# DLRM tower: nine tables by one-hot instead of eleven, compared three chunks at a time, and a paced row of gathers

## What is computed

```python
e = stack([tbl_f[ids[:, f]] for f in range(26)], axis=1)          # 512 x 26 x 128
c = concatenate([dense[:, None, :], e], axis=1)                   # 512 x 27 x 128
inter = einsum('bfd,bgd->bfg', c, c)[:, iu, ju]                   # 351 pairs, f < g
h = concatenate([dense, inter, dense], axis=1)                    # 607
h = maximum(h @ W_top1 + b_top1, 0)                               # 512
h = maximum(h @ W_top2 + b_top2, 0)                               # 256
y = h @ W_top3                                                    # 1
```

## Time and profile before

| | |
|---|---|
| median of 3 runs | 130.52 us (130.05 to 130.78) |
| the profiled execution | 131.74 us, of which the span of the profile is 129.6 us |
| TensorE busy | 111.9 us, 1026 matmuls |
| VectorE busy | 85.5 us, 168 instructions |
| ScalarE busy | 81.1 us, 172 instructions |
| GpSimd busy | 60.4 us, 68 instructions |
| DMA | 12.28 MB, mean 95 GB/s |

### The profile page before, as it was taken

How to read it: one execution, slowest core, us unless ns; L and a number is a source line. 1 busy time by engine, 2 the same in 40 slices (tenths; PEclk the granted TensorE clock), 3 DMA queues, 4 the chain that set the end, 5 groups by cost and what they waited for, 6 DMA issues and landing times.

```text
span 129.6 us, 2680 instructions
## 1 busy us (share of the span) xinstructions
PE 111.9 (86%) x1026; PEld 91.5 (71%) x1026; DVE 85.5 (66%) x168; ACT 81.1 (63%) x172; POOL 60.4 (47%) x68
## 2 busy tenths in 40 slices
PE   0389999999799999999696929999999986996892
PEld 0147776775667767758476919999798985995890
DVE  3379999999999999999991970952166032571001
ACT  6398198769888989999603750983167413582231
POOL 2478786485748771526667756656742000000000
PEclk9999999999999999999999995999999999999999
DMA  4937787574894636621111212112201000000000
GB/s 121 272 81 206 231 254 211 135 200 102 226 247 139 192 71 214 195 43 40 48 51 37 58 28 70 46 45 52 65 22 46 18 0 0 5 0 21 0 0 1
DMA packets 6681, 12.28 MB, mean 95 GB/s; under 512 B 2926, under 2 KB 3598, under 8 KB 6669
## 3 DMA queue, kind: packets, MB, share of 16 engines
q1 hardware_dynamic: 4605, 7.92, 22.3%
q0 software_dynamic: 1920, 3.94, 11.7%
q10 hardware_dynamic: 144, 0.26, 0.8%
HBM read 11.91 MB, written 0.00 MB: 92 GB/s over the span
## 4 chain that ended last, share of the span: by engine, by line
DVE 50%; PE 35%; issue 5%; DMA 4%; ACT 3%; SPq 2%; DVEq 0%
DVE hot L468 31%; PE ps L581 11%; DVE tab_lo L457 9%; PE ps L605 8%; DVE z L494 6%; PE ps L618 4%; PE ps L565 3%; DMA ids_i<-in_ids_dram 3%; PE ps L531 2%; DVE emb_t L486 2%; PE ps L551 2%; SPq L317 2%; PE ps L548 2%; ACT z L416 1%; DMA z<-z 1%
## 5 line engine op out<-in xcount | busy, mean ns | idle before, releaser
L342 POOL DMA_INDIRECT rows<-in_tbl_dram,ids_i x60 | 59.5, 992 | 36.9 <-DMA rows<-in_tbl_dram,ids_i 24.9
L468 DVE TENSOR_SCALAR hot<-ps,row_no 125x512 fp32r<-125x512 f32 x68 | 46.1, 748 | 1.0 <-PE ps L518 1.0
L551 PE MATMUL ps<-hot,tab_lo 125*128 125x512 f32 x92 | 38.0, 413 | 1.9 <-DVE tab_lo L457 1.9
L548 PE MATMUL ps<-hot,tab_hi 125*128 125x512 f32 x92 | 38.9, 423 | 0.8 <-ACT emb_t L389 0.8
L494 DVE COPY z<-ps 32x112 f32<-32x112 f32 (+1 forms) x64 | 16.5, 258 | 14.0 <-PE ps L581 13.2
L416 ACT COPY z<-ps 32x112 f32<-32x112 f32 (+1 forms) x64 | 15.2, 238 | 13.9 <-PE ps L581 13.2
L548 PEld LDWEIGHTS ps<-hot,tab_hi 125*128 125x128 f32 x92 | 18.4, 200 | 7.4 <-issue 2.1
L551 PEld LDWEIGHTS ps<-hot,tab_lo 125*128 125x128 f32 x92 | 18.3, 199 | 6.9 <-DVE tab_lo L457 3.2
L581 PE MATMUL ps<-emb_t 128*64 128x52 f32 x512 | 17.7, 232 | 4.8 <-DVE emb_t L486 3.6
L581 PEld LDWEIGHTS ps<-emb_t 128*64 128x64 f32 x512 | 17.0, 149 | 6.0 <-ACT emb_t L408 4.0
L605 PE MATMUL ps<-z,w_pair 128*128 128x128 f32 x128 | 16.6, 277 | 1.1 <-DMA z<-z 1.1
(11 more groups left out here) (42 smaller groups left out, 66.1 us busy)
## 6 DMA issues: line engine op xcount, KB each, us to landing
tab<-in_tbl_dram SPq DMA_DIRECT2D x9, 448.0 KB
tab<-in_tbl_dram SPq DMA_DIRECT2D x2, 560.0 KB
rows<-in_tbl_dram,ids_i POOLq DMA_INDIRECT x60, 3.1
w<-in_W_top_dram SPq DMA_DIRECT2D x1, 512.0 KB, 5.5
tab<-in_tbl_dram SPq DMA_DIRECT2D x9, 52.0 KB
x_rows<-in_r_dense_features_dram ACTq DMA_DIRECT2D x1, 256.0 KB, 3.3
w_x<-in_W_top_dram SPq DMA_DIRECT2D x1, 256.0 KB, 4.2
h_t<-in_W_top_dram SPq DMA_DIRECT2D x1, 256.0 KB, 4.5
```

Of the source, the lines that this page charges most:

```text
L342: pool.indirect_dma_start(out=rows[:, t, gathered.index(f), :], out_offset=None, in_=tables[f - 1], in_offset=bass.IndirectOffsetOnAxis(id ...
L468: nc.vector.tensor_scalar(hot[0:RP, k % OHB], ps[0:RP, IDV + n % 2, :], row_no[0:RP, row_cols(n, c)], None, ALU.is_equal).then_inc(hot_dve, 1)
L548: nc.tensor.matmul(bank, tab_hi[0:RP, n % SPLIT, c], one_hot, start=c == 0, stop=False)
L551: nc.tensor.matmul(bank, tab_lo[0:RP, n % SPLIT, c], one_hot, start=False, stop=c == CHUNKS[n] - 1).then_inc(hot_used, 1)
```

## The change

- Features 9 and 19 are gathered, not looked up by one-hot: 9 tables of 8 chunks remain; 17 features are gathered in 5 groups, 68 gathers. The groups are now (0 to 3), (12 to 15), (5 to 8), (9, 19, 20, 21), (23, 24).
- `ORDER`: g4 follows g3 in every tile, and g0:1 moves from between two tables to behind the last.
- VectorE compares chunks 0 to 2 and chunks 3 to 5 each in one `tensor_tensor` of 125 x 1536, with both inputs spread by a step of 0; the `tab_lo` of a table lies between the two. ScalarE builds chunks 6 and 7 (before: 3 and 6). One-hots have 16 buffers, two tables of 8.
- GpSimd waits at the head of each group for TensorE to have done a number of tables (group k of the whole row: k - 2 tables, up to 9), later for Gram units and first-layer blocks; the row of gathers in tiles 2 and 3 waits for the third before, not the second.

```diff
-ONEHOT = [4, 10, 11, 16, 17, 18, 22, 25, 26, 9, 19]
-GROUPS = [[(0, 4)], [(12, 4)], [(5, 4)], [(20, 2), (23, 2)]]
+ONEHOT = [4, 10, 11, 16, 17, 18, 22, 25, 26]
+GROUPS = [[(0, 4)], [(12, 4)], [(5, 4)], [(9, 1), (19, 3)], [(23, 2)]]
...
 ORDER = [
-    "h h g0:0 h g1:0 h g2:0 h g3:0 h h g0:1 h h h h",
-    "u0:0 g1:1 u1:0 g2-3:1 u0-1:1",
-    "g0-1:2 x0 l0-1:0 g2:2 l2-3:0 g3:2 e0 y0",
+    "h h g0:0 h g1:0 h g2:0 h g3:0 h g4:0 h h h",
+    "g0:1 u0:0 g1:1 u1:0 g2-4:1 u0-1:1",
+    "g0-1:2 x0 l0-1:0 g2:2 l2-3:0 g3:2 e0 g4:2 y0",
     "u0:2 x1 l0:1 u1:2 l1-3:1 g0:3 e1 g1:3 y1",
-    "x2 l0-1:2 g2-3:3 u0-1:3 x3 l2-3:2 e2 y2 l0-3:3 e3 y3",
+    "x2 l0-1:2 g2-4:3 u0-1:3 x3 l2-3:2 e2 y2 l0-3:3 e3 y3",
 ]
...
-    ACT_CHUNKS = [(3, 6) if m == R8 else (2, 5, 8) for m in CHUNKS]
-    DVE_CHUNKS = [tuple(c for c in range(m) if c not in a) for m, a in zip(CHUNKS, ACT_CHUNKS)]
-    OHB = 10
+    DVE_PARTS = [(0, 3), (3, 6)]
+    ACT_CHUNKS = (6, 7)
+    OHB = 2 * R8
...
-        return s[0] == "hot" or s[2] in ((1, 3) if s[1] == 0 else (0, 2))
+        return s[0] == "hot" or s[2] in ((1, 3, 4) if s[1] == 0 else (0, 2, 4))
...
@@ gpsimd @@
             for t in range(T):
-                for group in GROUPS:
+                for g, group in enumerate(GROUPS):
+                    tables_done = min(t * NG + g - 2, NH)
+                    if tables_done > 1:
+                        pool.wait_ge(hot_used, tables_done * R8)
+                    if t == 2 and g == 2:
+                        pool.wait_ge(gram_ps, NU)
+                    elif t == 2 and g == 4:
+                        pool.wait_ge(gram_ps, 2 * NU)
+                    elif t == 3 and g == 0:
+                        pool.wait_ge(l1_ps, NB // 2)
+                    elif t == 3 and g == 1:
+                        pool.wait_ge(l1_ps, NB)
+                    elif t == 3 and g == 3:
+                        pool.wait_ge(gram_ps, 3 * NU)
+                    elif t == 3 and g == 4:
+                        pool.wait_ge(l1_ps, 2 * NB)
                     for f in features(group):
                         if f:
-                            under_way = 4 if t < 2 else 2
+                            under_way = 4 if t < 2 else 3
...
@@ vector, build_hots @@
-                for m, c in enumerate(DVE_CHUNKS[n]):
-                    if m == 2:
+                for m, (c, end) in enumerate(DVE_PARTS):
+                    if m == 1:
                         split_lo(n)
-                    k = chunks_to(n) + c
-                    if k >= OHB:
-                        dve.wait_ge(hot_used, k - OHB + 1)
-                    nc.vector.tensor_scalar(hot[0:RP, k % OHB], ps[0:RP, IDV + n % 2, :], row_no[0:RP, row_cols(n, c)],
-                                            None, ALU.is_equal).then_inc(hot_dve, 1)
+                    if n >= 2:
+                        dve.wait_ge(hot_used, (n - 2) * R8 + end)
+                    shape = [RP, end - c, B]
+                    nc.vector.tensor_tensor(hot[0:RP, hot_at(n, c):hot_at(n, end)],
+                                            ps[0:RP, IDV + n % 2, :].unsqueeze(1).to_broadcast(shape),
+                                            row_no[0:RP, c:end].unsqueeze(2).to_broadcast(shape),
+                                            ALU.is_equal).then_inc(hot_dve, 1)
```

More of the change, by code:

```diff
@@ L86, in dlrm_tower, with hot_at @@
     assert D == P and N1 == BK and sorted(gathered + ONEHOT) == list(range(1, NF))
[L87 to L103, removed]
+    assert all(tables[f - 1].shape[0] == R8 * RP for f in ONEHOT) and w1.shape[0] == 2 * D + NPAIR
+    def hot_at(n, c):
+        return n % 2 * R8 + c
     steps = plan_steps()
@@ L168, in dlrm_tower @@
         ident_r = sb("ident_r", [NF - 1, NF - 1], F32R)
[L169 to L174, removed]
+        row_i = sb("row_i", [P, R8], I32)
+        row_no = sb("row_no", [P, R8])
+        neg_row = sb("neg_row", [P, R8])
+        tab = sb("tab", [P, RAW, R8, D])
+        tab_hi = sb("tab_hi", [P, SPLIT, R8, D], F32R)
+        tab_lo = sb("tab_lo", [P, SPLIT, R8, D], F32R)
         hot = sb("hot", [P, OHB, B], F32R)
@@ L358, in split_hi @@
                 if n >= SPLIT:
-                    act.wait_ge(hot_used, chunks_to(n - SPLIT + 1))
-                nc.scalar.copy(tab_hi[0:RP, n % SPLIT, 0:CHUNKS[n]], tab[0:RP, n % RAW, 0:CHUNKS[n]]).then_inc(hi_ready, 1)
+                    act.wait_ge(hot_used, (n - SPLIT + 1) * R8)
+                nc.scalar.copy(tab_hi[0:RP, n % SPLIT], tab[0:RP, n % RAW]).then_inc(hi_ready, 1)
             def build_hots(n):
@@ L371, in how_far @@
                     nc.scalar.activation(away[0:RP, a % 2], ps[0:RP, IDA + n % 2, :], ACT.Abs,
-                                         bias=neg_row[0:RP, row_cols(n, ACT_CHUNKS[n][m])]).then_inc(away_ready, 1)
+                                         bias=neg_row[0:RP, ACT_CHUNKS[m]:ACT_CHUNKS[m] + 1]).then_inc(away_ready, 1)
                 how_far(0)
-                for m, c in enumerate(ACT_CHUNKS[n]):
-                    if m + 1 < len(ACT_CHUNKS[n]):
+                for m, c in enumerate(ACT_CHUNKS):
+                    if m + 1 < len(ACT_CHUNKS):
                         how_far(m + 1)
-                    a = act_to(n) + m
-                    k = chunks_to(n) + c
+                    a = n * len(ACT_CHUNKS) + m
                     act.wait_ge(away_ready, a + 1)
-                    if k >= OHB:
-                        act.wait_ge(hot_used, k - OHB + 1)
-                    nc.scalar.activation(hot[0:RP, k % OHB], away[0:RP, a % 2], ACT.Relu, bias=1.0,
+                    if n >= 2:
+                        act.wait_ge(hot_used, (n - 2) * R8 + c + 1)
+                    nc.scalar.activation(hot[0:RP, hot_at(n, c)], away[0:RP, a % 2], ACT.Relu, bias=1.0,
                                          scale=-1.0).then_inc(hot_act, 1)
@@ L541, in _ @@
                     bank = ps[:, ROT + bank_of(s), :]
-                    for c in range(CHUNKS[n]):
-                        if c in ACT_CHUNKS[n]:
-                            pe.wait_ge(hot_act, act_to(n) + ACT_CHUNKS[n].index(c) + 1)
-                        else:
-                            pe.wait_ge(hot_dve, dve_to(n) + DVE_CHUNKS[n].index(c) + 1)
-                        one_hot = hot[0:RP, (chunks_to(n) + c) % OHB]
+                    for c in range(R8):
+                        if c in ACT_CHUNKS:
+                            pe.wait_ge(hot_act, n * len(ACT_CHUNKS) + ACT_CHUNKS.index(c) + 1)
+                        else:
+                            pe.wait_ge(hot_dve, n * len(DVE_PARTS) + sum(first <= c for first, _ in DVE_PARTS))
+                        one_hot = hot[0:RP, hot_at(n, c)]
                         nc.tensor.matmul(bank, tab_hi[0:RP, n % SPLIT, c], one_hot, start=c == 0, stop=False)
@@ L551, in _ @@
                         nc.tensor.matmul(bank, tab_lo[0:RP, n % SPLIT, c], one_hot,
-                                         start=False, stop=c == CHUNKS[n] - 1).then_inc(hot_used, 1)
+                                         start=False, stop=c == R8 - 1).then_inc(hot_used, 1)
                     if n + 2 < NH:
@@ L587, in _ @@
                     if t == 0:
-                        pe.wait_ge(hot_dve, dve_to(NH))
-                        pe.wait_ge(hot_act, act_to(NH))
+                        pe.wait_ge(hot_dve, NH * len(DVE_PARTS))
+                        pe.wait_ge(hot_act, NH * len(ACT_CHUNKS))
                         pe.wait_ge(w_x_ready, 1)
```

27 lines of the change are left out of this document (11 added, 16 removed).

## The result

The changed kernel took 125.82 us (median of 4 runs, 124.05 to 127.91) against 130.29 us for the kernel before (4 runs; the 130.52 ahead of the prediction is the median of three of them). The ratio, 0.9579 with a 95% interval of 0.9458 to 0.9699, is of fast runs alone, which leaves out those over 1.5% above the fastest, 127.91 and 126.16. The change is faster, as forecast, but by 4.5 us by the medians (5.5 by the ratio) and not 11.2; 119.3 was forecast, and 125.8 lies 1.3 above the end of the range. The profiled execution took 127.91 us, its span is 126.0. It is the longest of the four; a second profile, further down, tells which of its rows are usual.

What follows compares the result with a forecast made beforehand. TensorE and VectorE both bound the table stage, TensorE and its hand-overs with the copies what follows. -12.4 (tables) + 0.85 (g4) + 0.35 (late gather) = -11.2, so 130.5 becomes 119.3 us; range 117.6 to 124.5.

Steps and rivals of the forecast that it cites:

- The table stage: TensorE's tables, two removed: the stage ends at 55.45 us, 12.4 earlier, with TensorE and not VectorE as its bound.
- The 0.20 for slips: Table stage on TensorE: an allowance of 0.2 us for small slips in the sum that ends at 55.45.
- The 32nd to 37th at 1.4 come to about 56.7: GpSimd's gathers late in the table stage: 1.4 us each after the 31st at 48.27, the new waits costing nothing.
- a rival for the new instruction: Table stage: the joint comparison might hold gathers back as `tab_lo` does; chance 0.07, over half of it slower.
- two slips of the kernel before: TensorE's 0.8 us wait at 33 and slow Gram units at 77 (1.5 us); without both, 117.0 us.
- the rival of the late gathers: GpSimd behind 55 us: delayed gathers idle TensorE, whose clock may fall for 1.5 more; 121.5 to 125 us, chance 0.17.
- the gathers become the bound: GpSimd behind 55 us: no cushion left, so every gather delay reaches the end; 121.5 to 125 us, chance 0.17.
- just in time: End of the gather row: TensorE bound, g4:3 waiting only a little for its gather; 118 to 121 us, chance 0.6.
- VectorE as the bound: Table stage: the joint comparison saves nothing (1.98 us each), giving 120.9 us, or 128.5 at 2.4; chance 0.14.
- The lock by the joint comparison: Table stage: the joint comparison shuts gathers out, two or three a table; 133.1 or 122 us, chance 0.07.
- The waits of GpSimd for tables: Group heads in the table stage: each wait is met before GpSimd gets there, so they cost nothing.
- g4 cost: Later tiles: Gram unit 0 also waits for g4, 0.25 us each in tiles 1 and 3, 0.35 in tile 2, sum 0.85.

Runs made afterwards that it cites:

- f1: The changed kernel run again without an edit, on a chip of the first kind: 124.44 us beside 130.76 for the kernel before.
- f3: The changed kernel with features 23 and 24 gathered in tile 0 alone, 62 gathers for 68, first kind of chip: 120.1 us.
- f2: The changed kernel without any of GpSimd's waits for tables, Gram units and layers, first kind of chip: 123.46 us.
- h1: The changed kernel with `tab_lo` filled by a copy of the ids from PSUM, second kind of chip: 151.74 us beside 162.79 for the kernel before.
- e2: The changed kernel without any of GpSimd's waits for TensorE's progress, second kind of chip: 165.47 us.
- g1: The changed kernel without GpSimd's waits for TensorE and with six gathers under way for four and three, second kind of chip: 188.56 us.
- e1: The changed kernel run again without an edit, on a chip of the second kind: 148.37 us beside 162.16 for the kernel before.

## Why the prediction was wrong

**The table stage was right.** Two tables out, TensorE's own pitch (4.48 and 5.03), VectorE no longer a bound, 1.67 a comparison where 1.74 was taken: u0:0 at 55.8 (f1) or 58.2 (first profile) around the forecast 56.8. The 0.20 for slips was too sure. In the first profile the first table became 1.3 quicker (the pitch of its matmuls falls from 0.43 to 0.23 at 12.8 us, before at 15.6), table 4's load did not land sooner (ScalarE's `tab_hi` starts at 28.41, before at 28.28), so the wait in front of it grew from 0.80 to 2.16, and the clock behind it was 0.55: 1.6 more.

**The step that failed** is the one on GpSimd: "The 32nd to 37th at 1.4 come to about 56.7", from which the sum has the last gather start at 94.4. Two things are wrong in it.

*A step is lost in the count.* The 31st starts at 48.27; six steps of 1.4 give 56.67 as the start of the 37th. The 38th would follow at 57.9 and the last, 30 steps of 1.25 on, at 95.4. The sum goes by 56.9 and 94.4. By its own prices the forecast was 1.0 short, 120.3 us and not 119.3.

*The row in the table stage is slower than its price.* In f1 the 38th starts at 59.81, 1.9 behind 57.9. The 31st is at 49.54 for 48.27, and the next seven steps take 10.27 for 9.65. What lies in them is what a `tab_lo` or the fill does to a gather: beyond 0.94 each, gathers are stretched by 4.7 us in all ahead of the 38th in f1, 3.6 of it by `tab_lo` and 1.1 by the fill and the sum behind the last comparison, where before it was 1.9 ahead of the 31st, all of it inside the pace of 1.46. The waits for landings ahead of the 31st are alike (4.1 for 4.2). I had priced this very mechanism, from the row of 41.16, but only as a rival for the new instruction, and had left what the old ones do out of the sum. How many gathers start inside a `tab_lo` is chance: in the first profile the stretch ahead of the 38th is 3.9, and 5.9 go to waits for landings (4.5 in f1). This is worked out from the rows; no run on the first kind took the stretch away.

From the 38th to the last gather f1 runs as forecast: 37.68 for 37.5.

| | forecast | f1 | first profile |
|---|---|---|---|
| 38th gather starts | 56.9 | 59.81 | 60.55 |
| last gather starts | 94.4 | 97.49 | 100.73 |
| u0:3 starts | 98.4 | 101.27 | 104.68 |
| its 128 matmuls | 3.94 | 5.15 | 5.60 |
| span | 118.4 | 122.2 | 126.0 |

The first profile loses 2.7 more behind the 38th, at 71.20, 76.59, 86.09 and 94.49, where the third gather before landed 3.4 to 4.3 after its start: three under way were enough for the landing of 2.75 that I read in the earlier trace rows, but not for the slower ones. Three of the four are heads of groups, which also wait for TensorE's count and start 0.72 after the landing instead of 0.26; the sum had that second wait at nothing.

**What the lateness costs depends on TensorE.** The forecast left TensorE two slips of the kernel before, the wait of 0.80 at 33 and the slow Gram unit of 77.37, and said that without both it would be 117.0. In f1 both are gone (the wait is 0.20, the unit takes 3.94). From f3's chain (u0:3 32.8 behind u0:1, 1.55 of that the slow unit) I estimate that TensorE alone would have reached u0:3 at about 95.8 in f1; it starts at 101.27. So the gathers hold f1 up by some 5.5 us and 1.2 of clock, and f2, which has both slips, by 1.6 (101.13 beside f3's 99.50) and 1.6 of clock. What TensorE wins or loses ahead of the meeting point no longer shows in the time.

**The second term left out is the clock.** That a wait before u0:3 brings the lower clock was in the rival of the late gathers, at 1.5, and it comes with them: 1.2 in f1 (granted clock 0.74), 1.7 in the first profile (0.67). In f3, without the waits, it is 0.

So the rival "the gathers become the bound" (0.17) was what happened, and its 121.5 to 125 was about right for f1 (124.4). Its chance was too low: the forecast had TensorE and GpSimd meet within 0.4 us at g4:3, after 68 serial steps, and there any slip of the latter only adds; 0.6 for "just in time" was too much.

**The other rivals.** VectorE as the bound: no, it waits for TensorE 3.6 us in the stage. The lock by the joint comparison: no (f1, h1). The waits of GpSimd for tables: TensorE's count never came last in f1, as forecast, but the wait as such delays a head whose landing comes last; between 0 and 2 us on the first kind (f2). In the later tiles g4 cost 0.53 in tile 1 (u1:0 to u0:1 is 6.10, before 5.57) for 0.25, and 0.11 in tile 2 (g0:2 to u0:2, 9.34 for 9.23) for 0.35.

## What to carry to other kernels

Where a change moves work from the engine that bounds to a serial queue with slack, lay that queue out start by start under the new timing, and give the point where the two meet a range to one side: the slack lost is paid in full, with a fallen clock on top. Count its steps twice: one lost step was a third of the error at the 38th gather. What an existing instruction does to a neighbour (here each `tab_lo` to each gather that starts in it) belongs into the sum and not only into the rivals. And time such a change on more than one chip: here the same pacing was worth nothing that could be told from noise on one and 15 to 17 us on another.

## What the runs showed of the hardware

- On the chips of the second kind TensorE's matmuls come very slowly while GpSimd's gathers run, with no wait in the profile: one in 2.8 us beside a row of gathers 1.25 apart (e2), and 22 in 58 us with six under way (g1). With gathers held back, 64 of a Gram unit took 3.24 us at the lower clock (e1). The kernel before takes 162 to 165 us there for 130 on the first kind.
- A gather that starts inside a `tab_lo` (two SBUF inputs, 1.22 us) is held until about its end: 1.66 for 0.94 (f1). One already under way is not. A comparison or a copy with its wide operand in PSUM does nothing to it (0.95 in f1, 0.94 in h1). A fill of 128x1280, which has no input, holds it too: 2.47 over the fill and the sum behind it (f3).
- Where a gather's issue has two waits, for a landing and for a count, and the landing comes last, the chain of waits of the first profile shows it starting 0.72 after the landing (75.87 to 76.59) instead of 0.26 (85.83 to 86.09). Taking the second wait out brought the 38th gather 0.8 forward in f2, not the 1.8 of f1's four such heads: the rest was waited for at the next landing.
- The landing of a gather takes 2.4 to 7.3 us in the first profile, median 3.0.
- Equal waits need not bring an equal clock: ahead of u0:1 TensorE waited 1.64 and 0.92 us in f1 and went on at 1.00 (3.94 us), 1.64 and 0.88 in the first profile and went on at 0.69 (5.49 us). What decided it was not traced.
